# Two expert tables, VectorE's order in the choice part, and a third of the list's lanes on VectorE, in a two-layer decoder

## The chip, the cores and the metric

One core of one Trainium2 chip runs the whole program as a single launch. The metric is the device time of one execution in microseconds; the median of several executions is compared between kernels. The profiles show one execution each.

## The reference

The network is a decoder of two layers over `x` of 8 sequences, 512 positions and 256 features. The change touches one stage only, the routed experts of the first layer, in which 32 experts serve 4096 tokens and each token goes to 4 of them:

```python
xf = x.reshape(T, D)                          # T = 4096, D = 256
scores = softmax(xf @ Wg, axis=-1)            # E = 32
weights, indices = top_k(scores, 4)
for e in range(E):                            # capacity C = 2048
    pos = nonzero(pair_expert == e, size=C, fill_value=P)[0]
    tok = where(pos < P, pair_token[...], 0)
    out = swiglu(xf[tok], W1[e], W2[e], W3[e]) * w[:, None]
    y = y.at[tok].add(out)
z = swiglu(xf, Ws1, Ws2, Ws3)                 # the shared expert
return y + z
```

Around this stage stand two attention layers, a correlation mixer, a recurrence and a second expert layer (64 experts of 768 features), which the change leaves alone.

## The kernel before

The stage is `mix_experts_routed`. It has three parts, and in each of them every engine runs its own list of instructions, in the order in which the code writes them; engines meet only at semaphores.

**The choice part** goes over 8 batches `b` of 4 x 128 tokens. TensorE transposes the normalized rows (`turn`), forms the 32 logits (`logits`), counts ranks (`ranking`), and between these computes the shared expert of batch `w = b - 2`: `first` (L1755, tile `mr_s_hp`) and `second` (L1775, tile `mr_s_yp`). ScalarE copies the transposed rows, takes the exponentials and the silus (L1841). VectorE normalizes the rows of a later batch (`rows`, L1878, tile `mr_s_xg`), chooses the top 4 (`exponents`, `choice`), turns the counts into ranks (`ranking`, L1914 and L1915), multiplies the shared expert's halves (`hiddens`, L1945, tile `mr_s_hid`) and adds its output to `x` (`add`, L1952). `second` of TensorE waits for both `hiddens` of its batch. The order on VectorE within a batch is written in one loop: exponents, add, choice, ranking, rows, hiddens.

**The list part** makes a list of the tokens of each tile of 128 (160 tiles in all). For each of 32 groups of 128 tokens (`t`), a matrix of lanes and a matrix of tiles are built and multiplied on TensorE (L1813). The lanes are built in three steps in place: GpSimd subtracts (L1726), ScalarE squares (L1860) and takes a relu (L1863). VectorE builds the tiles' matrix (L1939). Both matrices have three slots (`ONES = 3`); slot `t % 3` is free when group `t - 3` has been multiplied (`listed`). Every 8 groups VectorE runs `placing`, which gives GpSimd its next lane numbers. The beginning of this part also turns counts into numbers of tiles (`first_rows`, L1959 and L1961).

**The tile part** is a loop over 160 tiles, 8 to a turn. GpSimd gathers the rows (`mr_e_xt`), TensorE transposes them (L2080, tile `mr_e_xp`), multiplies with W1 and W3 (L2094, `mr_e_hp`) and, three tiles later, with W2 (L2086, `mr_e_yp`). VectorE copies the weights of the tile's expert (L2134), forms `mr_e_hid` (L2156) and, four tiles later, weighs the output (L2149, `mr_e_y`). TensorE's W2 product of a tile waits for VectorE's `mr_e_y` of two tiles before. Which expert a tile has is read into registers, once a turn and engine, from the table `mr_expert_y`: VectorE reads 13 numbers that start at a multiple of 8, TensorE 8 numbers that start one place behind a multiple of 8, since its lag is 3 tiles and VectorE's 4:

```python
pe.load(regs_y, expert_y[0:1, bass.ds(i * UNROLL + UNROLL + LAG_O - LAG_Y, UNROLL)])
dve.load(now, expert_y[0:1, bass.ds(i * UNROLL, len(now))])
```

## Time and profile before

| | |
|---|---|
| median of 3 runs | 2622.28 us (2620.72 to 2623.58) |
| the profiled execution, its own time | 2614.44 us |
| span of the profiled execution | 2612.7 us |
| TensorE, busy share | 87% |
| VectorE, busy share | 52% |
| ScalarE, busy share | 32% |
| GpSimd, busy share | 35% |
| choice part, from the first logits to the counts | 378 to 504 us |
| list part | 504 to 582 us |
| tile part | 583 to 897 us |

The busy shares are means over the whole program. The stage that the change touches ends at 897 us of 2612.7; everything behind it starts when it has ended.

### The profile page before, as it was taken

How to read it: one execution, taken by the hardware profiler on the slowest of the kernel's cores; microseconds unless marked ns; L12 is line 12 of the kernel's file. 1: busy time of each engine (PE TensorE's matmuls, PEld its weight loads, DVE VectorE, ACT ScalarE, POOL GpSimd, SP SyncE). 2: the span in 40 equal slices, each digit the busy share in tenths (PEclk: the TensorE clock that was granted, in tenths of full speed). 3: DMA queues.
4: the chain of work that ended last, by engine and by line, in shares of the span. 5: the costliest groups of instructions: out<-in, count | busy, mean ns of one | idle time of the engine just before them, and what ended most of it. 6: DMA issues, size and time to landing. Idle time of an engine off the chain costs nothing. (4 is left out here: it accounts for less than half of the span.)

```text
span 2612.7 us, 40494 instructions
## 1 busy us (share of the span) xinstructions
PE 2263.5 (87%) x12436; PEld 1562.1 (60%) x12437; DVE 1366.6 (52%) x2986; ACT 825.1 (32%) x1755; POOL 916.0 (35%) x1089
## 2 busy tenths in 40 slices
PE   6999768878888755888888888899999999999997
PEld 3445445567787622334333333555669898899886
DVE  5554254565555555776677765369523333333332
ACT  2222312363232212555655566222111111111111
POOL 1100210164454444554444211122224444444443
PEclk9999879999999977999999999899999999999998
DMA  4000126004454634444334220510028888888885
GB/s 127 0 0 0 45 57 210 28 7 138 137 146 144 145 98 87 106 106 108 76 68 102 72 74 1 180 33 17 17 78 266 267 265 265 265 259 263 271 256 162
DMA packets 188868, 323.18 MB, mean 124 GB/s; under 512 B 29079, under 2 KB 141439, under 8 KB 188778
## 3 DMA queue, kind: packets, MB, share of 16 engines
q1 hardware_dynamic: 148586, 257.68, 30.2%
q0 software_dynamic: 40192, 64.42, 12.6%
q8 instruction: 43, 0.70, 0.1%
q14 instruction: 47, 0.39, 0.0%
HBM read 262.18 MB, written 59.23 MB: 123 GB/s over the span
## 5 line engine op out<-in xcount | busy, mean ns | idle before, releaser
L2725 PE MATMUL me_hp<-me_xgT,me_w 128*128 128x160 f32 x3072 | 435.8, 302 | 3.2 <-DMA me_w<-in_L_ffn_w_exp 2.3
L2725 PEld LDWEIGHTS me_hp<-me_xgT,me_w 128*128 128x128 f32 x3072 | 420.6, 191 | 26.6 <-issue 25.3
L1393 DVE TENSOR_REDUCE hd_nmax<-hd_wide 128x2 f32<-128x1024 f32 x256 | 307.6, 1219 | 127.4 <-PE hd_wide L1131 124.7
L1322 ACT ACTIVATE hd_prob<-hd_slim 128x512 f32<-128x512 f32 x512 | 276.2, 601 | 189.7 <-PE hd_slim L1142 153.7
L2793 DVE TENSOR_TENSOR me_hid<-me_act_out,me_hp 128x160 f32<-128x160 f32 x384 | 123.4, 321 | 336.0 <-ACT me_act_out L2749 295.4
L2749 ACT ACTIVATE me_act_out<-me_hp 128x160 f32<-128x160 f32 x384 | 116.8, 304 | 557.9 <-PE me_hp L2725 503.5
L1142 PE MATMUL hd_slim<-hd_q_stack,hd_k_stack 100*128 100x512 bf16 x512 | 199.5, 393 | 40.3 <-ACT hd_prob L1322 34.0
L1131 PE MATMUL hd_wide<-hd_k_stack,hd_q_stack 97*128 97x512 bf16 x512 | 200.5, 396 | 34.1 <-DVE hd_nmax L1393 16.1
L2042 POOL DMA_INDIRECT mr_e_xt<-routed_rows,mr_token x160 | 152.0, 950 | 160.2 <-DVE mr_e_y L2149 128.1
L2094 PEld LDWEIGHTS mr_e_hp<-mr_e_xtT,mr_e_w_now 128*128 128x128 f32 x1280 | 173.8, 197 | 8.7
L2094 PE MATMUL mr_e_hp<-mr_e_xtT,mr_e_w_now 128*128 128x128 f32 x1280 | 174.5, 281 | 0.0
L2380 PE MATMUL me_r_hp<-me_r_xnT,me_r_sw 128*128 128x512 f32 x384 | 167.8, 593 | 0.0
L1142 PEld LDWEIGHTS hd_slim<-hd_q_stack,hd_k_stack 100*128 100x128 bf16 x512 | 50.2, 99 | 194.6 <-ACT hd_prob L1322 86.5
L1014 POOL DMA_INDIRECT all_x<-outputs,rt_place x96 | 149.9, 1562 | 28.4 <-issue 28.2
L2638 POOL DMA_INDIRECT out_x<-me_oa,me_then_a x64 | 101.8, 1590 | 156.8 <-DMA out_x<-me_ob,me_then_b 111.2
L1154 PE MATMUL hd_pv<-hd_prob,hd_v 128*32 128x512 f32 x1024 | 137.7, 610 | 3.9 <-ACT hd_oT L1285 3.6
L2337 POOL TENSOR_TENSOR me_r_hid<-me_r_act_out,me_r_up_out 128x512 f32<-128x512 f32 x48 | 64.7, 1347 | 213.9 <-ACT me_r_up_out L2436 213.9
L2380 PEld LDWEIGHTS me_r_hp<-me_r_xnT,me_r_sw 128*128 128x128 f32 x384 | 72.5, 191 | 84.7 <-issue 84.3
L2086 PE MATMUL mr_e_yp<-mr_w,mr_e_hid 128*128 x320 | 103.3, 405 | 11.7 <-DVE mr_e_y L2149 10.2
L2156 DVE TENSOR_TENSOR mr_e_hid<-mr_e_act_out,mr_e_hp 128x128 f32<-128x128 f32 x160 | 45.9, 287 | 117.4 <-ACT mr_e_act_out L2119 78.1
L1131 PEld LDWEIGHTS hd_wide<-hd_k_stack,hd_q_stack 97*128 97x128 bf16 x512 | 50.3, 100 | 90.2 <-DVE hd_nmax L1393 29.1
L1726 POOL TENSOR_TENSOR mr_s_at_lane<-mr_s_lanes,mr_s_lane_f 128x512 f32<-128x512 f32 x32 | 46.7, 1483 | 160.0 <-DVE mr_s_lane_f L1931 148.3
(380 smaller groups left out, 3830.5 us busy)
## 6 DMA issues: line engine op xcount, KB each, us to landing
me_w<-in_L_ffn_w_exp SPq DMA_DIRECT2D x192, 512.0 KB
me_w_first<-in_L_ffn_w_exp SPq DMA_DIRECT2D x32, 768.0 KB
me_w_second<-in_L_ffn_w_exp SPq DMA_DIRECT2D x32, 768.0 KB
outputs<-mr_e_y SPq DMA_DIRECT2D x160, 128.0 KB
part_rows<-hd_parts SPq DMA_DIRECT2D x48, 256.0 KB
hd_k_stack<-part_rows SPq DMA_DIRECT2D x192, 64.0 KB
hd_q_stack<-part_rows SPq DMA_DIRECT2D x192, 64.0 KB
mr_w<-in_L_ffn_w_in SPq DMA_DIRECT2D x4, 2048.0 KB, 10.7
```

Of the source, the lines that this page charges most:

```text
L1014: nc.gpsimd.indirect_dma_start(out=x[:, r * TB + j, :], out_offset=None, in_=outputs[:, :], in_offset=bass.IndirectOffsetOnAxis(ap=place[: ...
L1131: last = nc.tensor.matmul(wide[:, at, j, :], q_stack[0:FIRST_ROWS, bt.slot, h, qc * P:(qc + 1) * P], k_stack[0:FIRST_ROWS, bt.slot, h, :], ...
L1142: nc.tensor.matmul(slim[:, slim_slot(bt, item), :], k_stack[:, bt.slot, h, kc * P:(kc + 1) * P], q_stack[:, bt.slot, h, :], start=True, st ...
L1154: last = nc.tensor.matmul(pv[32 * j:32 * j + 32, :], v[:, slot, kc, head(g, j), :], prob[:, kc * GH + j, :], start=(kc == 0), stop=(kc == ...
L1322: nc.scalar.activation(prob[:, u, :], slim[:, slim_slot(bt, item), :], ACT.Exp, scale=D ** -0.5)\
L1393: nc.vector.tensor_reduce(nmax[:, g % 2, n // 2, c:c + 2], wide[:, at], AX.X, ALU.max, negate=True)\
L2042: nc.gpsimd.indirect_dma_start(out=xt[:, n % UNROLL, :], out_offset=None, in_=rows_out[:, :], in_offset=bass.IndirectOffsetOnAxis(ap=token ...
L2094: last = nc.tensor.matmul(hp[:, v, half * P:(half + 1) * P], w_now[:, (u - LAG_H) % W_SLOTS, c, half * F:(half + 1) * F], xtT[:, v, c, :], ...
L2380: last = nc.tensor.matmul(hp[:, u % 2, half, :], sw1[:, c, at:at + P], xnT[:, c, b * S:(b + 1) * S], start=(c == 0), stop=(c == DC - 1))
L2725: last = nc.tensor.matmul(hp[:, f % 3, half * CAP:(half + 1) * CAP], w1[:, sl, c, cols], xgT[:, sl, c, :], start=(c == 0), stop=(c == DC - 1))
L2749: nc.scalar.activation(act_out[:, f % 2, :], hp[:, f % 3, CAP:2 * CAP], ACT.Silu).then_inc(silu_done, 1)
L2793: nc.vector.tensor_tensor(hid[:, sl, f, :], act_out[:, f % 2, :], hp[:, f % 3, 0:CAP], ALU.mult).then_inc(h_free, 1)
```

## The change

It has four pieces, in `mix_experts_routed` alone.

1. The table of experts exists twice: `expert_o` as before for VectorE, and `expert_y`, which starts one place later, so that TensorE's reads start at a multiple of 8 too.
2. In the choice part VectorE's order is exponents, rows, choice, add, hiddens, ranking.
3. Of the 32 groups of lanes, those with `t % 3 == 2` (10 of them) are built by VectorE in one comparison, ahead of that group's tile matrix; ScalarE then makes one relu of them in place of a square and a relu. GpSimd builds the other 22.
4. `first_rows` rounds the counts up with an addition and a shift on 32 columns, in place of a comparison and a sum over 512.

```diff
-        PER = CAP // P
         expert_y = k.sb("expert_y", [1, TILES + 2 * UNROLL], I32)
+        expert_o = k.sb("expert_o", [1, TILES + 2 * UNROLL], I32)
...
                     for t in range(NT):
+                        if t % 3 == 2:
+                            continue
                         pool.wait_ge(lanes_ready, t // GROUP + 1)
...
                     for t in range(NT):
-                        act.wait_ge(lane_off, t + 1)
                         lane = at_lane[:, t % ONES].rearrange("p n l -> p (n l)")
-                        nc.scalar.activation(lane, lane, ACT.Square).then_inc(lane_squared, 1)
-                        act.wait_ge(lane_squared, t + 1)
                         act.wait_ge(numbered, 1)
-                        nc.scalar.activation(lane, lane, ACT.Relu, bias=number[:, t:t + 1], scale=less_number[:, t:t + 1])\
-                            .then_inc(lane_numbered, 1)
+                        if t % 3 == 2:
+                            act.wait_ge(lane_even, t // 3 + 1)
+                            nc.scalar.activation(lane, lane, ACT.Relu, scale=number[:, t:t + 1]).then_inc(lane_numbered, 1)
+                        else:
+                            act.wait_ge(lane_off, t - t // 3 + 1)
+                            nc.scalar.activation(lane, lane, ACT.Square).then_inc(lane_squared, 1)
+                            act.wait_ge(lane_squared, t - t // 3 + 1)
+                            nc.scalar.activation(lane, lane, ACT.Relu, bias=number[:, t:t + 1], scale=less_number[:, t:t + 1])\
+                                .then_inc(lane_numbered, 1)
...
                         if t >= ONES:
                             dve.wait_ge(listed, t - ONES + 1)
+                        if t % 3 == 2:
+                            nc.vector.tensor_tensor(at_lane[:, t % ONES], lanes[:].unsqueeze(1).to_broadcast([P, TOP, P]),
+                                                    lane_f[:, t, :].unsqueeze(2).to_broadcast([P, TOP, P]), ALU.is_equal).then_inc(lane_even, 1)
...
-                        chain.link(nc.vector.tensor_tensor(over, count[:].unsqueeze(2).to_broadcast([P, E, PER]),
-                                                           steps_of[:].unsqueeze(1).to_broadcast([P, E, PER]), ALU.is_gt))
-                        chain.link(nc.vector.tensor_reduce(tiles[:], over, AX.X, ALU.add))
+                        chain.link(nc.vector.tensor_scalar(count_i[:], count[:], float(P - 1), None, ALU.add))
+                        chain.link(nc.vector.tensor_scalar(count_i[:], count_i[:], 7, None, ALU.arith_shift_right))
+                        chain.link(nc.vector.tensor_copy(tiles[:], count_i[:]))
...
                     for b in range(B):
                         exponents(b)
+                        if b + 2 < B:
+                            rows(b + 2)
+                        choice(b)
                         if b > LAG_W:
                             add(b - LAG_W - 1)
-                        choice(b)
-                        ranking(b)
-                        if b + 2 < B:
-                            rows(b + 2)
                         if b >= LAG_W:
                             for n in range(NS):
                                 hiddens(b - LAG_W, n)
+                        ranking(b)
...
-                    chain.tick(nc.vector.tensor_copy(expert_y[:], tp[0:1, 0:expert_y.shape[1]]))
+                    for dst, lag in ((expert_y, LAG_Y), (expert_o, LAG_O)):
+                        chain.tick(nc.vector.tensor_copy(dst[:], tp[0:1, LAG_O - lag:LAG_O - lag + dst.shape[1]]))
...
                         if not last_ones:
-                            pe.load(regs_y, expert_y[0:1, bass.ds(i * UNROLL + UNROLL + LAG_O - LAG_Y, UNROLL)])
+                            pe.load(regs_y, expert_y[0:1, bass.ds(i * UNROLL + UNROLL, UNROLL)])
...
-                        dve.load(now, expert_y[0:1, bass.ds(i * UNROLL, len(now))])
+                        dve.load(now, expert_o[0:1, bass.ds(i * UNROLL, len(now))])
```

On VectorE, between the exponents and the choice of batch 4, in the kernel before (`mr_s_lp` are the logits, `mr_s_xg` the normalized rows of batch 6, `mr_s_yp` the shared expert's output):

```order
L1884 TENSOR_REDUCE mr_s_nmax<-mr_s_lp 128x4
L1885 TENSOR_TENSOR mr_s_gates<-mr_s_lp,mr_s_nmax 128x128
L1952 TENSOR_TENSOR all_x<-all_x,mr_s_yp 128x512 x2
L1891 TENSOR_REDUCE mr_s_total<-mr_s_gates 128x4
L1892 RECIPROCAL mr_s_total<-mr_s_total 128x4
```

The same place with the change:

```order
L1889 TENSOR_REDUCE mr_s_nmax<-mr_s_lp 128x4
L1890 TENSOR_TENSOR mr_s_gates<-mr_s_lp,mr_s_nmax 128x128
L1883 TENSOR_SCALAR mr_s_xg<-all_x,all_mean,all_rstd 128x256 x4
L1896 TENSOR_REDUCE mr_s_total<-mr_s_gates 128x4
L1897 RECIPROCAL mr_s_total<-mr_s_total 128x4
```

The additions have left this place, and the rows of the later batch have come to it.

On VectorE at the end of the same choice, before (`mr_s_before` is the last result of the choice, `mr_s_lp` are now the ranks, `mr_s_hid` the shared expert's hidden products):

```order
L1906 TENSOR_SCALAR mr_s_chosen<-mr_s_left 128x128
L1908 TENSOR_TENSOR mr_s_before<-mr_s_before,mr_s_chosen 128x32 x4
L1914 SCALAR_TENSOR_TENSOR mr_s_chosen<-mr_s_lp,mr_s_chosen 128x128
L1915 SCALAR_TENSOR_TENSOR mr_s_ranked_rows<-mr_s_lp,mr_s_chosen 128x128
L1878 TENSOR_SCALAR mr_s_xg<-all_x,all_mean,all_rstd 128x256 x4
L1945 TENSOR_TENSOR mr_s_hid<-mr_s_act_out,mr_s_hp 128x512 x2
```

And with the change:

```order
L1911 TENSOR_SCALAR mr_s_chosen<-mr_s_left 128x128
L1913 TENSOR_TENSOR mr_s_before<-mr_s_before,mr_s_chosen 128x32 x4
L1960 TENSOR_TENSOR all_x<-all_x,mr_s_yp 128x512 x2
L1953 TENSOR_TENSOR mr_s_hid<-mr_s_act_out,mr_s_hp 128x512 x2
L1919 SCALAR_TENSOR_TENSOR mr_s_chosen<-mr_s_lp,mr_s_chosen 128x128
L1920 SCALAR_TENSOR_TENSOR mr_s_ranked_rows<-mr_s_lp,mr_s_chosen 128x128
```

The two hidden products stand ahead of the ranks, which close the batch.

On VectorE at the beginning of the list, groups 0 to 6, in the kernel before:

```order
L1945 TENSOR_TENSOR mr_s_hid<-mr_s_act_out,mr_s_hp 128x512 x2
L1939 TENSOR_TENSOR mr_s_at_tile<-mr_s_tile_nos,mr_s_tile_f 128x640 x5
L1952 TENSOR_TENSOR all_x<-all_x,mr_s_yp 128x512 x2
L1939 TENSOR_TENSOR mr_s_at_tile<-mr_s_tile_nos,mr_s_tile_f 128x640 x2
L1945 TENSOR_TENSOR mr_s_hid<-mr_s_act_out,mr_s_hp 128x512
```

And with the change:

```order
L1953 TENSOR_TENSOR mr_s_hid<-mr_s_act_out,mr_s_hp 128x512 x2
L1947 TENSOR_TENSOR mr_s_at_tile<-mr_s_tile_nos,mr_s_tile_f 128x640 x2
L1945 TENSOR_TENSOR mr_s_at_lane<-mr_s_lanes,mr_s_lane_f 128x512
L1947 TENSOR_TENSOR mr_s_at_tile<-mr_s_tile_nos,mr_s_tile_f 128x640 x3
L1960 TENSOR_TENSOR all_x<-all_x,mr_s_yp 128x512 x2
L1945 TENSOR_TENSOR mr_s_at_lane<-mr_s_lanes,mr_s_lane_f 128x512
```

A comparison for the lanes now stands ahead of every third tile matrix.

## Rows read from the trace of the kernel before

**Rows 1.** Waits of TensorE, 380 to 504 us: total us, times, longest

```profile
PE mr_s_yp L1775 <- DVE mr_s_hid L1945: 16.6, 6, 3.2
PE mr_s_tp L1736 <- DVE mr_s_xg L1878: 4.0, 2, 2.0
```

**Rows 2.** Timeline, batch 4: start us, duration, what, [idle before and releaser]

```profile
446.87 0.60 ACT L1841 ACTIVATE mr_s_act_out<-mr_s_hp 128x512 f32<-128x512 f32 x1 [4.43 <-PE mr_s_hp L1755]
446.89 0.39 PE L1765 MATMUL mr_s_lp<-mr_s_chosen,mr_s_tri 128*128 128x128 f32 x2
...
447.85 1.37 DVE L1878 TENSOR_SCALAR mr_s_xg<-all_x,all_mean,all_rstd 128x256 f32<-128x256 f32 x4
449.14 1.27 DVE L1945 TENSOR_TENSOR mr_s_hid<-mr_s_act_out,mr_s_hp 128x512 f32<-128x512 f32 x2
...
450.47 3.72 PE L1775 MATMUL mr_s_yp<-mr_s_sw,mr_s_hid 128*128 128x256 f32 x16 [3.19 <-DVE mr_s_hid L1945]
```

**Rows 3.** Timeline, `second` in batches 5 and 6

```profile
467.35 6.56 PE L1775 MATMUL mr_s_yp<-mr_s_sw,mr_s_hid 128*128 128x256 f32 x16 [3.19 <-DVE mr_s_hid L1945]
...
485.79 5.41 PE L1775 MATMUL mr_s_yp<-mr_s_sw,mr_s_hid 128*128 128x256 f32 x16 [1.90 <-DVE mr_s_hid L1945]
```

**Rows 4.** List part, one source line each: duration ns min/median/max

```profile
L1726 POOL TENSOR_TENSOR mr_s_at_lane<-mr_s_lanes,mr_s_lane_f x32: 1036/1617/1679, 510.4 to 576.7; 128x512 f32<-128x512 f32 x32
L1860 ACT ACTIVATE mr_s_at_lane<-mr_s_at_lane x32: 612/630/632, 511.8 to 578.3; 128x512 f32<-128x512 f32 x32
L1863 ACT ACTIVATE mr_s_at_lane<-mr_s_at_lane,mr_s_number,mr_s_less_number x32: 812/813/815, 512.4 to 579.0; 128x512 f32<-128x512 f32 x32
L1939 DVE TENSOR_TENSOR mr_s_at_tile<-mr_s_tile_nos,mr_s_tile_f x32: 810/882/1681, 512.5 to 576.5; 128x640 f32<-128x640 f32 x32
```

**Rows 5.** Timeline of the list part, single places

```profile
511.89 0.69 DVE L1945 TENSOR_TENSOR mr_s_hid<-mr_s_act_out,mr_s_hp 128x512 f32<-128x512 f32 x1 [0.90 <-ACT mr_s_act_out L1841]
...
562.11 1.35 PE L1813 MATMUL mr_s_lp<-mr_s_at_tile,mr_s_at_lane 128*128 128x160 f32 x8 [0.23 <-ACT mr_s_at_lane L1863]
...
564.41 3.98 DVE L1939 TENSOR_TENSOR mr_s_at_tile<-mr_s_tile_nos,mr_s_tile_f 128x640 f32<-128x640 f32 x3
```

**Rows 6.** Register loads from the table: ns min/median/max, one line each

```profile
L2140 DVEq TENSOR_LOAD <-mr_expert_y x21: 619/1094/1308, 583.0 to 897.0; - x21
L2158 DVEq TENSOR_LOAD <-mr_expert_y x1: 558/558/558, 582.3 to 582.3; - x1
L2099 PEldq TENSOR_LOAD <-mr_expert_y x20: 2026/2379/2663, 598.8 to 895.3; - x20
```

**Rows 7.** Waits of TensorE in the tile part, 586 to 905 us

```profile
PE mr_e_xp L2080 <- issue: 30.1, 19, 2.0
PE mr_e_yp L2086 <- DVE mr_e_y L2149: 10.2, 15, 0.8
```

**Rows 8.** Timeline at the end of one turn and the start of the next

```profile
614.90 1.05 PE L2094 MATMUL mr_e_hp<-mr_e_xtT,mr_e_w_now 128*128 128x128 f32 x8
...
617.95 0.43 PE L2080 MATMUL mr_e_xp<-all_ident,mr_e_xt 128*128 128x128 f32 x2 [1.99 <-issue]
...
618.30 0.48 DVE L2149 TENSOR_SCALAR mr_e_y<-mr_e_yp,mr_e_xt 128x256 f32<-128x256 f32 x1 [1.70 <-issue]
...
619.94 0.60 PE L2086 MATMUL mr_e_yp<-mr_w,mr_e_hid 128*128 x2
```

**Rows 9.** Timeline, start and middle of the turn before

```profile
601.21 0.43 PE L2080 MATMUL mr_e_xp<-all_ident,mr_e_xt 128*128 128x128 f32 x2 [0.88 <-issue]
...
603.26 0.69 PE L2086 MATMUL mr_e_yp<-mr_w,mr_e_hid 128*128 x2
...
608.83 0.69 PE L2086 MATMUL mr_e_yp<-mr_w,mr_e_hid 128*128 x2 [0.68 <-DVE mr_e_y L2149]
```

**Rows 10.** Windows of these two turns: stretch, length, busy of PE, PEld, DVE, ACT, POOL, then clock

```profile
598.80:614.70 15.90, 13.69 (x100) 12.32 (x99) 8.76 (x26) 5.09 (x18) 7.62 (x9) 1.00 0.52 152
614.70:629.60 14.90, 12.91 (x97) 12.01 (x96) 8.31 (x23) 4.40 (x14) 7.76 (x9) 1.00 0.50 146
```

More of the change, by code:

```diff
@@ L1660, in mix_experts_routed @@
             ones = k2.sb("ones", [P, P])
-            steps_of = k2.sb("steps_of", [P, PER])
             tile_no = k2.sb("tile_no", [P, 2])
-            over = at_tile[:, 0].rearrange("p n t -> p (n t)")[:, 0:E * PER].rearrange("p (e m) -> p e m", m=PER)
+            count_i = k2.sb("count_i", [P, E], I32)
             count = k2.sb("count", [P, E])
@@ L1682, in mix_experts_routed @@
             gated, lanes_ready, lane_off, lane_numbered = s.sem("gated"), s.sem("lanes_ready"), s.sem("lane_off"), s.sem("lane_numbered")
-            lane_squared, numbered = s.sem("lane_squared"), s.sem("numbered")
+            lane_squared, lane_even, numbered = s.sem("lane_squared"), s.sem("lane_even"), s.sem("numbered")
             tile_made, listed, tokens_ready = s.sem("tile_made"), s.sem("listed"), s.sem("tokens_ready")
@@ L1715, in _ @@
                                             pattern=[[1, P]], channel_multiplier=-1).then_inc(made, 1)
-                    for t, pattern, base, by_row in ((steps_of, [[P, PER]], 0, 0), (tile_no, [[P, 2]], -LAG_O, 1), (number, [[P, NT]], 0, 1),
+                    for t, pattern, base, by_row in ((tile_no, [[P, 2]], -LAG_O, 1), (number, [[P, NT]], 0, 1),
                                                      (lanes, [[1, P]], 0, 0), (tile_nos, [[1, TILES]], 1, 0)):
@@ L1719, in _ @@
                                        allow_small_or_imprecise_dtypes=True).then_inc(made, 1)
-                    pool.wait_ge(made, 7)
+                    pool.wait_ge(made, 6)
                     nc.gpsimd.tensor_scalar(less_number[:], number[:], -1.0, None, ALU.mult).then_inc(numbered, 1)
                     for t in range(NT):
+                        if t % 3 == 2:
+                            continue
                         pool.wait_ge(lanes_ready, t // GROUP + 1)
@@ L1980, in _ @@
                     chain.wait()
-                    dve.wait_ge(made, 7)
+                    dve.wait_ge(made, 6)
                     for b in range(B):
                         exponents(b)
+                        if b + 2 < B:
+                            rows(b + 2)
+                        choice(b)
                         if b > LAG_W:
                             add(b - LAG_W - 1)
-                        choice(b)
-                        ranking(b)
-                        if b + 2 < B:
-                            rows(b + 2)
                         if b >= LAG_W:
@@ L2098, in steps @@
                         if not last_ones:
-                            pe.load(regs_y, expert_y[0:1, bass.ds(i * UNROLL + UNROLL + LAG_O - LAG_Y, UNROLL)])
-                    pe.load(regs_y, expert_y[0:1, LAG_O - LAG_Y:LAG_O - LAG_Y + UNROLL])
+                            pe.load(regs_y, expert_y[0:1, bass.ds(i * UNROLL + UNROLL, UNROLL)])
+                    pe.load(regs_y, expert_y[0:1, 0:UNROLL])
                     steps(0, True, False)
@@ L2156, in steps @@
                                 nc.vector.tensor_tensor(hid[:, (u - LAG_H) % 4, :], act_out[:, v, :], hp[:, v, P:2 * P], ALU.mult).then_inc(hid_ready, 1)
-                    dve.load(regs[0:1], expert_y[0:1, LAG_O:LAG_O + 1])
+                    dve.load(regs[0:1], expert_o[0:1, LAG_O:LAG_O + 1])
                     weights(regs[0], 0)
```

## The prediction

> **What bounds the stage now.** I first asked for the waits of TensorE in each of the stage's three parts, since TensorE is the busiest engine, then for the timeline around the longest wait of each part. Everything after the stage starts when it has ended, so a microsecond off its length is one off the kernel.
>
> In the choice part TensorE waits 16.6 us in 6 pieces for VectorE's hidden products, and 4.0 us in 2 pieces for normalized rows [rows 1]. The timeline of batch 4 shows why [rows 2]: TensorE's ranking ends at 446.89 + 0.39 = 447.28. ScalarE's second silu ends at 447.47, so both hidden products could be made then; but VectorE first turns the ranks, then normalizes the rows of batch 6 (1.37 us), then makes both products (1.27 us), and TensorE's `second` starts at 450.47, 3.19 us late. The list part is a ring of three slots through GpSimd, ScalarE and TensorE [rows 4, 5]. In the tile part TensorE stands 30.1 us in 19 pieces, one at each turn, with nothing that holds it but its own instruction issue, and 10.2 us in 15 pieces for VectorE's output of an earlier tile [rows 7]. What is issued there is the read of 8 expert numbers, which takes 2.03 to 2.66 us [rows 6].
>
> **The choice part.** In the new order the ranks and the rows no longer stand ahead of the hidden products. The first product (half of 1.27) can be made when the first silu is there, long before. The second one starts when the second silu ends, 447.47, plus 0.04, takes 0.69 [rows 5], and releases TensorE at about 448.25. The wait becomes 448.25 - 447.28 = 0.97 us, so 2.22 us go. Rows 1 gives 16.6 us in 6 waits: four with rows to normalize (batches 2 to 5) at 3.19 each are 12.8, and the two last batches, which have none, make the other 3.8 (one is the 1.90 of [rows 3]). Their wait also falls to 0.97. Together 4 x 2.22 + 2 x 0.93 = 10.7 us.
>
> The two waits of 2.0 us for rows are those of batches 0 and 1, where the 1.37 us of rows stand behind the ranking that TensorE has just finished. Ahead of the choice they are done some 9 us earlier. The lower bound of what goes is those 1.37 us (ScalarE's copies wait for the exponents, which move up by that much), the upper one is 2.0; I take 1.7 each, 3.4 together.
>
> What is late next: the additions now stand behind the choice, and TensorE needs them before the next `second`, 16 us later; they take 1.3 us and are hidden. The choice gets 1.37 us of rows ahead of it, but no longer waits for `second` as the additions did; the ranking on TensorE needs its result only some 5 us after it is there. If that cover went, the loss would be 1.37 us a batch. Rows that are normalized earlier need their slot stored: the store was issued three batches before. So this part gives 10.7 + 3.4 = 14.1 us. Bounds: 9 (if half of the four large gains met another wait) and 16.
>
> **TensorE's clock in the choice part.** Behind two of the six waits `second` ran at the lower of its two levels for a while: 6.56 and 5.41 us where the same 16 matmuls take 3.72 [rows 2, 3]. That is 2.84 + 1.69 = 4.5 us. With waits of 1 us in place of 3.2 these falls may go or come elsewhere. Bounds 0 and 4.5; I take the middle, 2.3 us.
>
> **The list part.** A slot that GpSimd fills passes through 1.62 us of GpSimd, 0.63 + 0.81 of ScalarE and 1.35 of TensorE, with some 0.2 of hand-overs: 4.6 us, for three groups 1.54 each [rows 4, 5]. ScalarE's own time is 0.63 + 0.81 + 0.14 = 1.58 a group. The change takes ScalarE's load down to about (2 x 1.58 + 0.9)/3 = 1.35, but two of the three slots keep their whole ring of 1.54, and VectorE gets 10 comparisons. Such a comparison is not in the trace; the nearest rows are VectorE's 0.69 us for 128x512 [rows 5], and for a tile matrix of 128x640 0.81 alone and 3.98/3 = 1.33 beside GpSimd [rows 4, 5], so 0.69 to 1.1 each, 7 to 11 us in all, for the engine that also has `placing` to do while the others wait. I take 0 for the sum of both, with 32 x (1.58 - 1.35) = 7 us of gain as one bound, cut to 4 because two slots keep their ring, and 4 us of loss as the other (a third of the 11 us falls where TensorE waits for VectorE anyway). Here a rule bears. Beside GpSimd three tile matrices took 3.98 us and not 3 x 0.81 = 2.4, while GpSimd's subtraction rose from 1.04 to 1.62. The Trainium skill (SBUF — State Buffer, "Who interferes with whom") says that the port pair which both share is an exclusive lock. By that rule each group would cost 0.81 + 1.04 in turn, and a comparison of 0.69 on VectorE for one of 1.04 on GpSimd would save 10 x 0.35 = 3.5 us. The rows show less than a lock, since GpSimd got about two and a half of its operations done in those 3.98 us.
>
> `first_rows` loses about 0.8 us on VectorE. It is hidden: the hidden product behind it waits 0.90 us for ScalarE anyway [rows 5]. The second table costs one more copy on one partition while VectorE waits for the list's end, nothing.
>
> **The tile part.** VectorE reads 1 number in 0.56 us, 8 in 0.62 (the shortest of the 21, the last turn's) and 13 in 1.1 to 1.3, all from aligned places; TensorE reads 8 in 2.03 to 2.66 from one place further on [rows 6]. The trace has no aligned read by TensorE. Bounds: 0.62 as VectorE's, and 2.4 if the engine and not the place makes it slow. I take about 1, since number and place are both known to be cheap on VectorE.
>
> A short read doesn't give all of the 30.1 us back. After a long wait of 1.99 us, TensorE's second W2 product of the turn starts at 619.94, while the output it needs was ready on VectorE at 618.30 + 0.48 = 618.78: 1.1 us can go there [rows 8]. That time hangs on VectorE's own read. After a short wait of 0.88 us the product starts at 603.26, and only about 0.2 can go [rows 9]. The mean wait is 30.1/19 = 1.58; between the two cases that is 0.2 + (1.58 - 0.88)/(1.99 - 0.88) x 0.9 = 0.77 us a turn, 15 us for 19.
>
> Against this stands what the turns themselves show. The turn with the short wait took 15.9 us, the one after the long wait 14.9 [rows 10], for in the first TensorE was stopped in the middle for outputs of VectorE (0.68 us at 608.83 [rows 9]). The time spent at the read is partly time in which ScalarE and VectorE catch up. If each turn got two such stops of 0.68, 19 x 1.36 = 26 us would stand where 10.2 do, and the 15 would be given back whole. I take half: 7.4 us. Bounds 0 and 17 (with the clock's falls after the long waits gone as well).
>
> **Sum.** 14.1 + 2.3 + 0 + 7.4 = 23.8 us off. The profiled execution took 2614.4 us, 1.7 more than its span, and the median of the runs is 7.8 above it; on its own time the sum gives 2590.6, on the median 2622.3 - 23.8 = 2598.5.
>
> **Rivals.**
> - The tile part gives nothing, because the read is no shorter or because the stops in the turn take it all. For it speaks [rows 10]. Time: 2622.3 - 16.4 = 2605.9. The mechanism in the kernel would be that each number costs TensorE about 2.38/8 = 0.3 us wherever it lies. Against that speak VectorE's 13 numbers in 1.1 us, under 0.09 each. The Trainium skill (Runtime: NRT & Kernel Launch, "Instruction fetch mechanics") gives some 200 ns for each register read, in bulk too, but for reads from HBM; by that rule alignment would change nothing here and the sum would be the 16.4 us of this rival.
> - The tile part gives its 15 us whole and the clock's falls go: 14.1 + 4.5 + 15 + 2 = 36, so 2587. For it: most of the waits are long ones.
> - The list grows because VectorE becomes its bound: all 11 us of comparisons on the path. VectorE's median of 0.88 for a tile matrix leaves room in 2 us a group, which speaks against. Time: 2622.3 - 23.8 + 11 = 2609.5.
> - Slower: TensorE's clock stays at 1.2 GHz longer in the choice part. At that level `second` took 6.56/3.72 = 1.76 times as long; a batch of 16.9 us has 13.7 us of TensorE's work, so each batch more at that level costs 10.4 us. It decides from the third batch on: 23.8 - 31.2 gives 2629.7. Against it: with waits of 3.19 us in every batch the clock fell for parts of two batches only, and the waits get shorter.
>
> **Chances.** Forecast (about half of the tile part's gain) 0.45; nothing from the tile part 0.27; all of it 0.20; the list grows 0.05; slower by the clock 0.03. The likeliest one's own range is 2591 to 2604. Range: from the case that gives all, with 4 us from the list, 2583, up to the list's or the tile part's loss with the choice part at its lower half, 2613. A change of 0.2%, 5 us, is about what a measurement of this kernel can tell from none. Faster by more: 0.93. Within it: 0.05. Slower: 0.02.
>
> **What the new profile would show.** Choice part: TensorE's waits for the hidden product at 0.9 to 1.0 us each, those for rows gone, `second` at 3.72 us in each batch, the part 14 to 18 us shorter. List part: 0.69 to 1.1 us for the new comparison, the part's length within 4 us of now. Tile part: TensorE's read near 1 us or below, the waits at a turn's start from 30 down to below 12 us, and waits for VectorE's outputs risen from 10 to some 18 us. Wrong would be the forecast if the read kept its 2.4 us, if the stops inside the turns grew beyond 25 us or stayed at 10, if the hidden products still came 3 us late, or if the list's ring were held by VectorE.

## The result and the profile after

The changed kernel takes 2592.57 us (median of 4 runs, 2591.68 to 2593.76), the kernel before beside it 2622.93 (2620.72 to 2633.20). The ratio is 0.9877, with a 95% interval of 0.9851 to 0.9903: 30.4 us less by the medians, where 23.8 were forecast. The profiled execution of the changed kernel took 2591.68 us with a span of 2589.8, which is 22.9 less than the span of the one before. So some 7.5 of the 30.4 us are no difference of the two traces: the profiled execution of before, at 2614.44, lay 8.5 us under the median of 2622.93 with which the changed kernel is compared, that of the changed kernel 0.9 under its own. Of all executions below, one of r6_yp4 took 4081.7 us at a granted clock of 0.675, where the others of that kernel had 0.951 to 0.959; it is left out of that kernel's median and ratio, and nothing here explains it.

Windows over the three parts of the stage give the division. The columns are stretch, length, busy time of TensorE with its instructions, granted clock, DMA share and GB/s. The stretches run from the first transpose to the matmul that makes the counts (choice part), on to the cast of the tokens (list part), and on to the last W2 product (tile part). That product ends at 901.6 us in the kernel before; the 897 us given as the stage's end ahead of the prediction are the start of VectorE's last register read [rows 6]. Before:

```profile
374.02:503.97 129.95, 104.84 (x417) 0.84 0.40 134
503.97:581.23 77.26, 63.89 (x325) 0.96 0.00 1
581.23:901.60 320.37, 272.52 (x1920) 0.97 0.51 138
```

And after:

```profile
374.92:485.68 110.76, 99.91 (x416) 0.88 0.46 159
485.68:563.67 77.99, 63.91 (x325) 0.93 0.00 1
563.67:880.00 316.33, 271.39 (x1920) 0.97 0.54 140
```

The choice part lost 19.2 us, the list part gained 0.7, the tile part lost 4.0. Of the choice part the waits of TensorE (total us, times, longest) read, after:

```profile
PE mr_s_tp L1737 <- DVE mr_s_xg L1883: 14.8, 3, 12.7
PE mr_s_yp L1776 <- DVE mr_s_hid L1953: 5.8, 6, 1.0
```

The 12.7 us are the stage's first rows, which were waited for before too (12.0 us). Of the two later waits of 2.0 us for rows [rows 1] one is gone and one stands at 1.3 (the third, of 0.8, was there before as a wait for ScalarE's copy). The six waits for the hidden product fell from 16.6 us [rows 1] to 5.8. The timeline of one batch shows the new order:

```profile
454.10 0.60 ACT L1842 ACTIVATE mr_s_act_out<-mr_s_hp 128x512 f32<-128x512 f32 x1 [4.43 <-PE mr_s_hp L1756]
454.12 0.39 PE L1766 MATMUL mr_s_lp<-mr_s_chosen,mr_s_tri 128*128 128x128 f32 x2
...
454.73 0.69 DVE L1953 TENSOR_TENSOR mr_s_hid<-mr_s_act_out,mr_s_hp 128x512 f32<-128x512 f32 x1 [4.34 <-ACT mr_s_act_out L1842]
455.33 0.28 DVE L1919 SCALAR_TENSOR_TENSOR mr_s_chosen<-mr_s_lp,mr_s_chosen 128x128 f32<-128x128 f32 x1
```

The silu ends at 454.70, the product starts 0.03 later with nothing ahead of it on VectorE, and the ranks are turned behind it (this is the second product; the first was made before these lines). Where rows 2 had 3.19 us of wait, `second` now waits 0.96. `second` takes 3.72 us behind every one of these waits, also in the two batches where it took 6.56 and 5.41 [rows 3]. In the grouped lines of this part it falls from 26.8 to 22.3 us of busy time.

In the tile part the register reads (minimum, median, maximum in ns) and TensorE's and ScalarE's waits are now:

```profile
L2108 PEldq TENSOR_LOAD <-mr_expert_y x20: 587/786/1058, 581.4 to 875.2; - x20
```

```profile
L2149 DVEq TENSOR_LOAD <-mr_expert_o x21: 614/1285/1294, 565.5 to 877.1; - x21
```

```profile
ACT mr_e_act_out L2128 <- issue: 75.9, 52, 2.5
...
PE mr_e_yp L2095 <- DVE mr_e_y L2158: 34.3, 43, 3.1
...
PE mr_e_xp L2089 <- DMA mr_e_xt<-routed_rows,mr_token: 9.3, 4, 4.8
```

TensorE's read fell from 2.38 us [rows 6] to 0.79, and with it all 30.1 us of its waits at the turns' start [rows 7] are gone. But its waits for VectorE's outputs rose from 10.2 us in 15 pieces to 34.3 in 43. One by one in the timeline, 19 of them are that for the first output behind VectorE's own read, 16.6 us together, and 24 lie at other places of a turn, 17.7 us together.

### The profile page after: what moved, and what is told of

It is laid out like the page before. It is cut to its first block and busy times, and to the rows that moved or that the text cites. A ratio compares the mean times of both kernels' runs of the same rounds, so it can differ in the third digit from the quotient of the medians.

```text
span 2589.8 us, 40477 instructions
## 1 busy us (share of the span) xinstructions
PE 2261.4 (87%) x12436; PEld 1560.0 (60%) x12437; DVE 1370.8 (53%) x2998; ACT 813.9 (31%) x1745; POOL 900.1 (35%) x1078
## 5 line engine op out<-in xcount | busy, mean ns | idle before, releaser
L2346 POOL TENSOR_TENSOR me_r_hid<-me_r_act_out,me_r_up_out 128x512 f32<-128x512 f32 x48 | 64.5, 1345 | 213.7 <-ACT me_r_up_out L2445 213.7
L2095 PE MATMUL mr_e_yp<-mr_w,mr_e_hid 128*128 x320 | 103.1, 405 | 35.4 <-DVE mr_e_y L2158 34.3
L2128 ACT ACTIVATE mr_e_act_out<-mr_e_hp 128x128 f32<-128x128 f32 x160 | 44.5, 278 | 202.9 <-PE mr_e_hp L2103 126.9
L2165 DVE TENSOR_TENSOR mr_e_hid<-mr_e_act_out,mr_e_hp 128x128 f32<-128x128 f32 x160 | 45.7, 286 | 114.0 <-ACT mr_e_act_out L2128 76.8
```

## The experiments

Each set of kernels ran on one chip, with the kernel before beside it, and the chips differ: in the first set the kernel before took 2573.5 us (median), in the other three 2624.9, 2615.3 and 2614.2. It was profiled on none of them, only in its first comparison. Times are therefore compared within a set, and the parts by the traces, read as above:

```
us                 choice   list    tile    time, median   ratio to before (95% interval)
set 1, before                              2573.5
r1_order            110.9   76.9   292.0   2552.5         0.9911 (0.9889 to 0.9934)
r2_aligned          131.4   78.7   289.4   2571.4         0.9994 (0.9978 to 1.0010)
r3_no_lanes         111.0   77.1   288.1   2552.1         0.9914 (0.9891 to 0.9938)
r4_shifted          110.7   77.9   352.9   2616.6         1.0150 (1.0123 to 1.0177)
set 2, before                              2624.9
r5_after_again      110.7   77.9   313.5   2586.1         0.9866 (0.9840 to 0.9891)
r6_yp4              110.8   78.0   309.2   2585.0         0.9853 (0.9827 to 0.9879)
r7_split_read       110.9   76.4   310.0   2584.2         0.9849 (0.9824 to 0.9875)
r8_half_lanes       110.8   76.8   320.1   2591.7         0.9867 (0.9842 to 0.9892)
set 3, before                              2615.3
r10_act_loop        110.8   76.5   304.0   2586.4         0.9892 (0.9867 to 0.9918)
r11_yp4_split       110.8   78.0   308.7   2580.8         0.9869 (0.9847 to 0.9891)
r12_order_again     110.9   76.9   323.6   2595.3         0.9931 (0.9904 to 0.9959)
set 4, before                              2614.2
r13_no_gathers      110.8   76.5   285.7   2564.0         0.9815 (0.9783 to 0.9846)
```

**One part of the change at a time.** r1_order is the kernel before with

```diff
                     for b in range(B):
                         exponents(b)
+                        if b + 2 < B:
+                            rows(b + 2)
+                        choice(b)
                         if b > LAG_W:
                             add(b - LAG_W - 1)
-                        choice(b)
-                        ranking(b)
-                        if b + 2 < B:
-                            rows(b + 2)
                         if b >= LAG_W:
                             for n in range(NS):
                                 hiddens(b - LAG_W, n)
+                        ranking(b)
```

> The kernel before with VectorE's new order in the choice part alone. The two traces read alone (theory A): from the first transpose to the counts the changed kernel needs 110.8 us where before needed 130.0, so this part alone should give 19 us off, 2604, with the hidden-product waits at 0.97 and every second product at 3.72 us. Rival B: part of the 4.5 us of lower clock comes back (it fell by chance), then 14 to 16 us off. The tile part should stay at 320 us in both.

It took 21.0 us less than the kernel before, and its choice part 110.9 us. The 4.5 us of clock came with it, so rival B falls. The falls of the clock come with the old order and not by chance: in r2_aligned, which has the old order too, `second` took 6.49, 5.21 and 5.41 us in three of the six batches, while in r1_order, r3_no_lanes, r5_after_again, r12_order_again and r13_no_gathers it took 3.72 in all six. What the theories did not have is the tile part: 292.0 us, where the same code took 320.4 in the first trace. That goes with the set and not with the order of VectorE, as the next kernels of the set show (288.1 and 289.4 us), and as r12_order_again does below.

r2_aligned is the kernel before with the second table and both reads aligned (lines of the change):

```diff
+                    for dst, lag in ((expert_y, LAG_Y), (expert_o, LAG_O)):
+                        chain.tick(nc.vector.tensor_copy(dst[:], tp[0:1, LAG_O - lag:LAG_O - lag + dst.shape[1]]))
-                            pe.load(regs_y, expert_y[0:1, bass.ds(i * UNROLL + UNROLL + LAG_O - LAG_Y, UNROLL)])
+                            pe.load(regs_y, expert_y[0:1, bass.ds(i * UNROLL + UNROLL, UNROLL)])
```

> The kernel before with the two aligned tables alone. The profiled executions differ by 4.0 us in the tile part, but the medians of the kernels differ by 7.5 us more than their profiles. Theory A: the other executions of the kernel before are longer than its profiled one somewhere that the change doesn't touch; then the tables give 4 us, 2619. Theory B: what they are longer by lies in the tile part, where a turn is held by the long read or not; then the tables give about 11 us, 2612. Both expect TensorE's read of 8 near 0.8 us.

2.1 us less by the medians, which the measurement can't tell from nothing; 2.6 by the tile parts of r1 and r2, 3.9 by those of r1 and r3. That fits theory A's 4 us and not theory B's 11. A's reason, that the executions of before are longer somewhere else, is not tested by it. The traces say why a read that is 1.6 us shorter gives so little even here, where nothing else disturbs a turn. Waits of TensorE in r1_order:

```profile
PE mr_e_xp L2080 <- issue: 24.0, 19, 1.5
...
PE mr_e_yp L2086 <- DVE mr_e_hid L2156: 1.5, 1, 1.5
PE mr_e_yp L2086 <- DVE mr_e_y L2149: 0.8, 1, 0.8
```

And in r3_no_lanes, which has the aligned tables:

```profile
PE mr_e_yp L2086 <- DVE mr_e_y L2149: 20.6, 20, 1.2
```

The 24.0 us for its own read turned into 20.6 us for the output that VectorE makes behind its read of 13 numbers, once a turn. TensorE had spent at its own read the time that it would have waited there anyway. Here there are no stops in mid-turn, in either kernel.

r3_no_lanes is the changed kernel with the three `t % 3 == 2` branches taken out (GpSimd makes all lanes again, ScalarE squares all of them).

> The changed kernel with all lanes made by GpSimd again. Theory A (the traces: the list part took 77.3 us before and 78.0 after): the comparisons on VectorE gain nothing, 0 to 2 us less without them, 2591 to 2592.5. Rival B (GpSimd and VectorE exclude each other, so a comparison of 0.69 for one of 1.04 saves 0.35 each): 3.5 us more without them, 2596.

The list part took 77.1 us. Over all kernels it took 76.9 to 78.7 with none of the lanes on VectorE, 76.4 to 78.0 with a third. Rival B's 3.5 us were not seen. The fourth piece of the change, the rounding in `first_rows`, was not run alone; r3_no_lanes has it and r1_order doesn't, and their list parts are 77.1 and 76.9 us. r8_half_lanes gives VectorE every second group:

```diff
+            LK = 2
-                        if t % 3 == 2:
+                        if t % LK == LK - 1:
                             continue
```

> The changed kernel with every second group of lanes made by VectorE in place of every third: 16 comparisons. The list part took 77.1 to 77.3 us with none and 78.0 with 10. Theory A (the ring of three slots sets the pace, and VectorE's comparisons beside GpSimd cost 1.0 to 1.5 us each): a little longer still, 78 to 80. Rival B (the engines' load sets it, and GpSimd and ScalarE were the bound): 2 to 4 us shorter, 74 to 76.

76.8 us: neither the loss of theory A nor the gain of B. Who makes the lanes doesn't matter within the 2.3 us by which the part varies. In the timeline of r5_after_again the six comparisons that met no subtraction of GpSimd took 0.68 to 0.69 us, the four that did 1.52 to 1.53 (minimum, median, maximum in ns):

```profile
L1945 DVE TENSOR_TENSOR mr_s_at_lane<-mr_s_lanes,mr_s_lane_f x10: 680/694/1527, 493.8 to 554.1; 128x512 f32<-128x512 f32 x10
```

r8's tile part, whose code is that of r5, took 320.1 us where r5's took 313.5, on the same chip. So much does this part vary, and a single trace tells nothing smaller.

**What makes a read slow.** r4_shifted is the changed kernel with

```diff
-                        dve.load(now, expert_o[0:1, bass.ds(i * UNROLL, len(now))])
+                        dve.load(now, expert_o[0:1, bass.ds(i * UNROLL + 1, len(now))])
```

and the table copied one number further on.

> The changed kernel with VectorE's table one number further on, so that its reads of 13 start one place behind an aligned one, as TensorE's reads of 8 did before. Theory A, the place makes the read slow, per number (2.38 / 8 = 0.30 us): 13 take 3.9 us in place of 1.29, some 2.6 us at each of 20 turns, all of it on TensorE's path, since it waits for the first output behind this read: 50 us more, 2643. Theory A', the place costs a fixed 1.6 us a read: 2.9 us, 32 us more, 2625. Theory B, the engine makes it slow: the read stays at 1.29 and the time at 2593.

```profile
L2149 DVEq TENSOR_LOAD <-mr_expert_o x21: 1850/2948/3140, 563.7 to 910.7; - x21
...
L2167 DVEq TENSOR_LOAD <-mr_expert_o x1: 550/550/550, 563.0 to 563.0; - x1
```

The engine theory falls: on VectorE, too, the place makes the read slow. 13 numbers take 2.95 us (A' said 2.9), the last turn's 8 take 1.85, and one alone 0.55. (That one lies at place 5 here and at place 4 in every other kernel, so neither of them starts at a multiple of 8, though the prediction calls all of VectorE's reads aligned; it takes 0.55 to 0.56 us in both.) That is 0.55 and about 0.2 us for each further number: (2.95 - 0.55) / 12 and (1.85 - 0.55) / 7. The fixed price of A' is wrong, its number was luck. The Trainium skill (Runtime: NRT & Kernel Launch, "Instruction fetch mechanics") gives some 200 ns per register, in bulk too, for reads from HBM, of which the stage has none. The reads from the shifted table come near this figure; the aligned reads of 8, with medians of 0.59 to 0.79 us, don't.

The price was far above both: 64.5 us over r3_no_lanes by the medians, 64.8 by the tile parts, for reads that grew by 20 x 1.86 = 37 us. TensorE's waits for the output grew by 35.0 (55.6 in 19 pieces, the longest 3.1 us), and its busy time by 29.6. The windows of r4_shifted and of r3_no_lanes:

```profile
561.90:914.80 352.90, 290.08 (x1920) 0.89 0.45 126
```

```profile
562.10:850.10 288.00, 260.52 (x1920) 0.99 0.58 154
```

The granted clock fell from 0.99 to 0.89 over the part. In the trace of r4_shifted it stood at its lower level, 0.50, for 78.5 us, in a stretch beside each of the 19 long waits and one at the part's start; in r3_no_lanes, whose longest wait of this kind is 1.2 us, for the 6.8 us at the start alone. The second half of the price is the clock's.

**The changed kernel again, on a chip like the first.**

> The changed kernel itself, for a second profile and for the comparison with the kernels that run beside it. By the parts of the traces so far (choice part 110.8 against 130 to 131, list 78.0 against 77.1, tile part 3.5 to 4 less) it should be 22 to 23 us below the kernel before. The other view, from the medians of its first comparison, is 30 us below.

38.8 us below by the medians, more than both views; its trace, with the tile part at 313.5, says 3 us more than the first one. No trace of the kernel before was taken on this chip, so where the rest lies is not shown. r12_order_again, r1's kernel on such a chip, divides it:

> The kernel before with VectorE's new order in the choice part alone, a second time, since its first runs were made on a chip where the tile part is 28 us shorter. Choice part 110.8 us, that is 19 to 20 less. On a chip where the kernel before takes 2620 us, theory A (order and tables are worth the same there): 19 to 21 us below the kernel before, which leaves 10 to 17 of the changed kernel's 30 and 39 us to the tables. Theory B (the moved order also moves the program's code, and with it ScalarE's late starts): more than 25 us below, or less than 15.

20.1 us below: theory A. Its tile part (misaligned reads) is 323.6 us, against 320.4 in the first trace of before; with aligned reads it is 313.5, 316.3 and, in r8_half_lanes, 320.1. So on these chips the tables are worth 0.3 to 10.1 us by the traces, and what the medians leave for them (30.4, 38.8 or, for r8_half_lanes, 33.1, less 20.1) is 10 to 19. These differences go across chips; the tables alone were run only in set 1.

**Taking VectorE's read off TensorE's path.** r6_yp4 gives the W2 product four places in PSUM:

```diff
-            yp = k2.ps("yp", [P, 2, S])
+            YB = 4
+            yp = k2.ps("yp", [P, YB, S])
...
-                dve.sem_inc(y_ready, 2)
+                dve.sem_inc(y_ready, YB)
```

> The changed kernel with four places for the W2 product in PSUM in place of two, so that TensorE need not wait at each turn for the first output that VectorE makes behind its own read. Theory A (this output bounds the turn, which is why the aligned table gave 4 us and not 15 or 30): TensorE's waits for the outputs (20 to 34 us in the tile part) fall below 5 and the tile part gets 15 to 20 us shorter. Rival B: the hidden product or the weights' copy, which stand behind the same read on VectorE, are late next: TensorE waits for them in its place, and 0 to 8 us are gained.

```profile
PE mr_e_yp L2096 <- DVE mr_e_hid L2166: 29.9, 36, 1.3
```

Rival B: the waits for outputs are gone, and those for the hidden product stand in their place. The tile part is 4.3 us shorter than r5's, which is within its spread. r7_split_read:

```diff
-                        dve.load(now, expert_o[0:1, bass.ds(i * UNROLL, len(now))])
+                        dve.load(regs[0:UNROLL], expert_o[0:1, bass.ds(i * UNROLL, UNROLL)])
...
+                            if u == 3 and not last_ones:
+                                dve.load(regs[UNROLL:], expert_o[0:1, bass.ds(i * UNROLL + UNROLL, LAG_O + AHEAD)])
```

> The changed kernel with VectorE's read of 13 numbers made in two: 8 at the turn's start, 5 ahead of the fourth tile of the turn. The last turn's read of 8 took 0.62 us where 13 take 1.09 to 1.32. Theory A (the length of the read at the turn's start is on TensorE's path): each turn's wait shortens by 0.5 to 0.7 us, and the second read, some 0.9 us with its start, fits into the slack in mid-turn: 8 to 13 us off the tile part. Rival B: the second stop is paid too: no gain, or up to 8 us more.

```profile
L2148 DVEq TENSOR_LOAD <-mr_expert_o x21: 602/606/631, 562.8 to 868.0; - x21
L2152 DVEq TENSOR_LOAD <-mr_expert_o x20: 602/742/818, 572.1 to 858.1; - x20
```

The read at the turn's start halved, TensorE's waits for outputs fell from 37.1 to 26.2 us, and the tile part from 313.5 to 310.0: less than A's 8, and too little to be told from B's nothing, with 6.6 us between r5's and r8's traces of the same code. Both edits together, r11_yp4_split:

> The changed kernel with both edits of the tile part together: four places for the W2 product, and VectorE's read made in two, of 8 and of 5. Theory A (on the slower chips ScalarE's late starts fill the turn whatever the rest does): like each edit alone, the tile part at 308 to 311 us and the time within 3 us of theirs. Rival B (the two add up): 302 to 305. On a chip where the kernel before takes 2573 us nothing but VectorE's read stands in the turn, and the two edits should take 1.2 of the 1.48 us that a turn is longer than its eight tiles of 1.545: the tile part from 288 to about 266.

308.7 us, theory A: the two don't add up. Neither edit nor their sum can be told from the changed kernel by the medians. Something else fills the turns. What the two edits would give where no silu is late was not run.

**What fills them.** In the changed kernel a timeline shows it at the end of a turn:

```profile
612.48 1.05 PE L2103 MATMUL mr_e_hp<-mr_e_xtT,mr_e_w_now 128*128 128x128 f32 x8
...
613.29 0.94 POOL L2051 DMA_INDIRECT mr_e_xt<-routed_rows,mr_token  x1 [0.60 <-issue]
...
614.70 0.28 ACT L2128 ACTIVATE mr_e_act_out<-mr_e_hp 128x128 f32<-128x128 f32 x1 [1.91 <-PE mr_e_hp L2103]
...
615.22 0.48 DVE L2158 TENSOR_SCALAR mr_e_y<-mr_e_yp,mr_e_xt 128x256 f32<-128x256 f32 x1
...
615.95 0.48 PE L2095 MATMUL mr_e_yp<-mr_w,mr_e_hid 128*128 x1 [0.55 <-DVE mr_e_y L2158]
```

The matmuls that this silu reads end at 612.48 + 1.05 = 613.53, its last instruction long before; it starts at 614.70, 1.1 us later than it could (the next one follows its matmuls by 0.07 us), with nothing in the trace that holds it. VectorE stands behind it, and TensorE behind VectorE. Counted from the traces, of the 160 silus start more than 0.5 us late: 22 in the kernel before, 33 in the changed one, 35 in r5, 30 in r12, 20 in r7, 44 in r6, 33 in r8, 36 in r11, and none in the four kernels of the first set. In the changed kernel 33 of the 38 starts of ScalarE that fell due 0.2 to 0.3 us after a gather had begun were late, and 1 of the 49 in the next 0.1 us. In r3_no_lanes of set 1 some 90 starts fell due in that same interval, and none was late. r10_act_loop changes ScalarE's code alone:

```diff
-                        for u in range(UNROLL):
-                            n = i * UNROLL + u
+                        for u in range(ACT_TILES):
+                            n = i * ACT_TILES + u
```

> The changed kernel with ScalarE's loop over the tiles in turns of 2 tiles in place of 8 (the same activations and waits in the same order; only the engine's code is shorter and its loop is closed four times as often). In the changed kernel on the chips where the kernel before takes 2620 us, ScalarE starts two of the 8 silus of a turn 1.1 to 1.3 us late, with nothing that holds it, and TensorE's waits in mid-turn follow from that. Theory A (it is ScalarE's own code that comes late at fixed places of its loop: the late ones are always those of the turn's 3rd and 6th tile, but lie elsewhere in kernels whose code differs): the late starts go or come at other places, and if they go, the tile part falls from 314 to 316 us to about 290. Rival B (they come when a silu is ready 0.2 to 0.3 us after GpSimd has begun a gather, where 33 of 38 were late): the same number of late starts, 38 to 45, and no change of time. On a chip where the kernel before takes 2573 us there are none, and both expect no change.

35 late silus, at the same two tiles of TensorE's turn although ScalarE's own turn now has two tiles: theory A falls. At one of them they come 0.62 us late in the mean where r5 had 1.06. The tile part was 304.0 us, lower than rival B had it, while the ratio to before is no better than the changed kernel's in set 2. r13_no_gathers leaves out the gathers of tiles 8 to 159, and so a part of the computation; GpSimd issues a small transfer in the place of each:

```diff
+                            nc.gpsimd.dma_start(xt[0:1, n % UNROLL, 0:1], rows_out[0:1, 0:1]).then_inc(x_loaded[n % UNROLL], 16)
+                            continue
                         nc.gpsimd.indirect_dma_start(out=xt[:, n % UNROLL, :], out_offset=None, in_=rows_out[:, :],
```

> The changed kernel without the gathers of tiles 8 to 159: GpSimd, at the same points and after the same waits, issues a transfer of one number in their place, so that the tiles work on the rows of the first eight (a part of the computation is left out). On the chips where the kernel before takes some 2620 us, 38 to 48 of ScalarE's starts in the tile part come 1.1 us late, and a shorter loop on ScalarE did not change that. Theory A (GpSimd's gathers, or what they move, make ScalarE's starts late): the late starts fall below 5, TensorE's waits for VectorE's outputs from 34 to 37 us down to the 20.6 us of the other chip, and the tile part from 314 to 316 us to 282 to 288. Rival B (something else on these chips does): some 40 late starts and a tile part of 308 us or more.

Theory A. Idle time of ScalarE before its silus and who ended it, in the tile part of the changed kernel, of r13_no_gathers, and of r3_no_lanes on the chip of set 1:

```profile
L2128 ACT ACTIVATE mr_e_act_out<-mr_e_hp 128x128 f32<-128x128 f32 x160 | 44.5, 278 | 202.9 <-PE mr_e_hp L2103 126.9 <-issue 75.9
```

```profile
L2130 ACT ACTIVATE mr_e_act_out<-mr_e_hp 128x128 f32<-128x128 f32 x160 | 44.4, 278 | 176.4 <-PE mr_e_hp L2105 176.4
```

```profile
L2119 ACT ACTIVATE mr_e_act_out<-mr_e_hp 128x128 f32<-128x128 f32 x160 | 44.3, 277 | 176.7 <-PE mr_e_hp L2094 176.7
```

One silu is late (in the first turn), TensorE's waits for outputs are 18.4 us in 21 pieces, once a turn, and the tile part is 285.7 us, 28 to 31 less than the changed kernel's two traces. It has the shape of set 1, where the gathers run and no silu is late. No kernel with gathers was profiled on this chip; that it is one of those with late silus is read from its kernel before (2614.2 us) and from its part behind the stage (742 us, see the end). GpSimd still issues at the same points, 0.52 us each where a gather takes 0.95, so not every issue of GpSimd's makes a silu late; the gather's own issue and the rows that it moves went together and are not told apart.

## Why the prediction was right, step by step

The total was right, and the choice part by its mechanism. That the sum of the traces came within 1 us of the forecast is partly luck: the choice part gave 2.8 us more than forecast, while the list part cost 0.7 and the tile part gave 3.4 less. In the tile part the half that is given back was a guess between two bounds, and its reason holds only in part.

- **Hidden products: 10.7 us.** Measured 16.6 - 5.8 = 10.8, each wait at 0.96 or 0.97 as forecast. The prediction's own terms add up to 447.47 + 0.04 + 0.69 = 448.20 and a wait of 0.92; the other 0.05 has no term there.
- **Rows: 3.4 us.** The waits ahead of the transposes fell by 3.4 (grouped lines: 18.3 less the first 12.0, against 15.6 less the first 12.7). The waits for rows were to be gone, though, and one of 1.3 us stayed; a wait of 0.8 for ScalarE's copy, which had no term, went in its place.
- **Clock in the choice part: 2.3 us.** It gave its upper bound, 4.5, and in every run of the new order (110.7 to 111.0 us for the part in twelve profiles). The middle between the bounds was too careful: the falls came with the old order both times that it was profiled, and in none of these twelve. With some 0.5 more the part lost 19.2 us where 16.4 were forecast.
- **List part: 0.** +0.7 in the traces, and within 2.3 us whoever makes the lanes. TensorE waited there 12.2 us for lanes that GpSimd begins, 0.4 for those that VectorE begins and never for a tile matrix, so VectorE did not become the bound. A comparison took 1.02 us in the mean, within 0.69 to 1.1. The exclusive lock of the Trainium skill (SBUF — State Buffer, "Who interferes with whom") would have given 3.5 us, as the prediction worked it out; no run shows them, though a comparison that met GpSimd took 1.53 us, near the 0.69 + 1.04 of one after the other.
- **Tile part: 7.4 us.** 4.0 in the two profiles, 0.3 to 10.1 over those of such chips. The read came down to 0.79 us (about 1 was said). The waits divide nearly as worked out: 30.1 us at the turns' start became 16.6 behind VectorE's read, a gain of 13.5 where 15 was said (below 12 was expected to stay), and the stops in mid-turn rose from 10.2 to 17.7 (some 18 was said). In the first trace the waits for the gathered rows rose too, from 6.1 to 9.3 us, but in r5_after_again, the same kernel, they took 6.0; that is spread and no cost of the change. What failed is the reason for the half. The engines behind TensorE were to need its pause to catch up, yet in set 1 the pause went and no stop in mid-turn came; there 24.0 us at the read became 20.6 behind VectorE's, so 3 to 4 us could go and not 15. Where stops do come, it is ScalarE's late starts beside GpSimd's gathers that they wait for, 22 silus in the kernel before and 33 in the changed one. So the size came out near the half on the chips with late silus, for a reason that the prediction did not have, and in set 1 the tables gave less than it: 2.1 us by the medians, 2.6 and 3.9 by the traces.
- **The sum on the median.** By the traces 22.9 us, forecast 23.8. The medians differ by 30.4, and 7.5 of that is that the profiled execution of before was a short one. The same code's tile part took 320.4 and 323.6 us in two profiles, so part of those 7.5 us may lie there; where they lie stays open.

Of the rivals, "the tile part gives nothing" is refuted in its mechanism (each number costs the same wherever it lies) by r4 and by the aligned read. "All of it" would need VectorE's read off the path and ScalarE's starts in time; r6, r7 and r11 did the first without the second and got 3.5 to 4.8 us by the traces, and no kernel had both, so this is argued and not shown. The slower case was real, only elsewhere: r4's waits of 3 us per turn did bring the clock down. What is not settled is why a gather makes ScalarE late on some chips and not on others, and whether it is the gather's issue or its transfer.

## What to carry to other kernels

A wait on an engine's own instruction is worth only what remains before the next engine's product arrives: look up when that product is ready, behind its own reads, before booking the wait as a gain. Put tables that registers are read from where each read starts at a multiple of eight numbers: one place off cost some 0.2 us a number on VectorE and some 0.3 on TensorE, while eight numbers in place cost no more than some 0.6 to 0.8 us in all. A read of 13 can be split into 8 and 5, which leaves 0.61 us in front in place of 1.29; that this shortens the kernel was not shown here. Where the clock fell behind long waits that a reordering takes away, book the fall with the waits and not at half: here it went with them in all twelve profiles. And compare kernels within one chip, since the chips differed here by more than the change is worth.

## What had not been expected of the hardware

Two kinds of chip show up for the same kernel, the one before: 2573 us, with no late silu in the four kernels profiled beside it, and 2614 to 2625, with 20 to 44 of 160 silus more than 0.5 us late in the part where GpSimd gathers. The attention part behind the stage, which no kernel changed, also differs: 725 to 728 us from its first matmul to the first of the second expert layer on the first chip, 736 to 742 on the others. No chip served for two of the sets, so whether it is the chip or only how it was at that time is not shown. And a read of one number costs 0.55 us although it starts off a multiple of eight, less than the 0.59 us and more of eight in place; off their place, only the numbers beyond the first are dear.
